# AdaLN and FFN adapters: a fixed first adapter, its first pieces and A's rows loaded in parts, ScalarE's small transfers later

## The chip, the cores and the metric

The kernel runs on one core of a Trainium2 chip. The metric is the device time of one execution in microseconds (us); lower is better. TensorE (PE in the profile) multiplies matrices, VectorE is DVE, ScalarE ACT, GpSimd POOL, and SyncE (SP) only issues transfers. A queue such as SPq or ACTq is the part of an engine that issues transfers and loads registers.

## The reference

For 64 samples of 64 tokens and 1024 features, two layers are applied, each added to its input:

```python
# layer 0
h = einsum('bct,bcd->bdt', x, L0_cond_weights[ids_0_15])       # mixes a sample's 64 tokens
y = h @ W_base.T + b_base + top-2-of-8 routed rank-16 adapters(h)
x = x + y
# layer 1
g = einsum('bsi,boi->bso', x, L1_cond_weight[ids_3_7])         # one of 8 matrices of 1024 x 1024 for each sample
z = 16 * sum over 8 heads of softmax(g @ Wr.T + br)[h] * (g @ A[h].T) @ B[h].T   # H = 8, scaling 2
x = x + z
```

Layer 1 never needs g itself: it needs g @ A.T and g @ Wr.T. So the kernel computes, once for each adapter in use, the product of [A; Wr] (136 rows of 1024) and the adapter's 1024 x 1024 matrix. This is the fold. The adapter numbers lie between 3 and 7, so five of eight are in use.

## The kernel before, in words

**The fold** (the first 82 us). The work on an adapter is cut in KC = 8 pieces. Piece c needs 512 KB of weights, `w1[KC*e + c]`, in the staging slot `stage[:, c, :]`, and all of [A; Wr]'s rows, `ag1_raw` (544 KB, eight blocks `oc` of 136 columns). TensorE makes 8 matmuls for it, one for each oc, with 128 columns of the piece and block oc of `ag1_raw` (`fold`, L391 to L403); in the trace each is two instructions. They sum in one of BANKS = 4 PSUM banks, and `unit_done` counts finished pieces (it starts at 8). ScalarE copies each result twice (`take_unit`, L629): rounded into `adapter` and unrounded into `hg`, then counts `unit_copied` (it starts at 4). TensorE waits at piece c for `unit_copied` >= 8n + c + 1, that is, for the copy of the piece four earlier. GpSimd subtracts one from the other to get the low part (L1065, `folded_lo`), and after four pieces ScalarE waits for that and stores the half adapter to device memory, `folded` (`take_adapter`, L638 to L645, signalled by `folded_stored`). The copies of the next adapter wait for these stores.

**Which adapters, in which order.** The first is the adapter of sample 0, read from `ids` by SP and ScalarE (`first_adapter`, L236). While it is folded, VectorE works out the list of the others in 14 short steps (L741 to L765, `plan_step`); every engine then reads how many there are and loops over them (`adapters_in_use`, L229, `adapter_at`, L233, each a register load).

**SP's order** (L342 to L372): the adapter ids, [A; Wr]'s rows whole, the register load of the first adapter, piece 0 in two halves (semaphores `first_landed` and `unit_landed[0]`), pieces 1 to 7, a wait for ScalarE's three small transfers (`small_landed`), then in the loop each piece once TensorE is done with its slot. After the fold's pieces come x of round 0, four of the eight mixing weights (`load_wc`), g0, the base weights in halves, and the turned x.

**ScalarE's order** (L620 to L698): three small transfers (condition ids, `br` and the bias, 0.2 to 4 KB), the load of its function table with one small exp, a wait for the three, four mixing weights `load_wc` (each a register load from `ids` and a transfer of 16 KB), then the first adapter's copies and stores, then the loop.

**TensorE** (L541 to L548) starts with WARM = 24 transposes of the identity matrix, waits for [A; Wr]'s rows, and folds. Behind the fold stand the mixing of round 0 (`mix`, L415), the gates, and eight rounds of the two layers.

Of the kernel before, what the change touches and what calls it, by code (L numbers as in the profile page):

```python
# [9 lines left out]
F32 = mybir.dt.float32  # L10
# [7 lines left out]
P = 128  # L18
SAMPLES = 64
CH = 64  # L20
D = 1024
KC = D // P
TOKENS = SAMPLES * CH
T = 512
# [4 lines left out]
EXPERTS = 8  # L29
RANK = 16  # L30
HR = EXPERTS * RANK
HG = HR + EXPERTS
# [3 lines left out]
BANKS = 4  # L36
SLOTS = 3
HALF = KC // 2
WARM = 24
REST = 4  # L40


# [5 lines left out]
def build(nc, x, x_turned, cond_ids, adapter_ids, w_cond, w0, g0, bias, b0, w1, ag1, b1, br, folded, out):  # L48
    with ExitStack() as ctx:
# [6 lines left out]
        def sem(name):  # L56
            return ctx.enter_context(nc.semaphore(name))
# [32 lines left out]
        adapter = sb("adapter", [P, SLOTS, KC, 2, HG], F32R)  # L90
# [12 lines left out]
        bias_cols = sb("bias_cols", [P, KC], F32)  # L103
        br_rows = sb("br_rows", [P, EXPERTS], F32)
        expert_no = sb("expert_no", [P, EXPERTS], F32)
        ids = sb("ids", [1, 2 * SAMPLES], I32)
# [48 lines left out]

        ids_landed = sem("ids_landed")
        small_landed = sem("small_landed")
        ag1_landed = sem("ag1_landed")
        first_landed = sem("first_landed")
        unit_landed = [sem(f"unit_landed{s}") for s in range(STAGE)]  # L160
        unit_done = sem("unit_done")
        unit_copied = sem("unit_copied")
# [69 lines left out]

        def adapter_at(eng, n):  # L233
            return eng.value_load(plan[0:1, bass.ds(n, 1)], min_val=0, max_val=EXPERTS - 1)

        def first_adapter(eng):  # L236
            eng.wait_ge(ids_landed, 16)
            return eng.value_load(ids[0:1, SAMPLES:SAMPLES + 1], min_val=0, max_val=EXPERTS - 1)

        def tail_out(n):  # L240

# [3 lines left out]
        def load_wc(eng, q, r, samples=range(PER)):  # L245

            for i in samples:
                no = eng.value_load(ids[0:1, bass.ds(at(q, r, PER, i), 1)], min_val=0, max_val=CONDS - 1)
                half = slice((i % 2) * CH, (i % 2 + 1) * CH)
                eng.dma_start(wc[half, i // 2, half], w_cond[bass.ds(no, 1), :, :].rearrange("a p n -> (a p) n")  # L250
                              ).then_inc(wc_landed, 16)
# [35 lines left out]
        def _(sp):  # L287
            def load_unit(e, c):
                sp.dma_start(stage[:, c, :], w1[bass.ds(KC * e + c, 1), :, :].rearrange("a p n -> (a p) n")
                             ).then_inc(unit_landed[c], 16)  # L290

            def load_x(q, r):
                for t in range(TILES):
                    sp.dma_start(x_rows[:, t, :], x[bass.ds(at(q, r, TILES, t), 1), :, :].rearrange("a p n -> (a p) n")
                                 ).then_inc(x_landed, 16)
# [43 lines left out]
                    load_xT(q, r + 1, 0)  # L339
                    load_xT(q, r + 1, 1)  # L340

            sp.dma_start(ids[:, SAMPLES:], adapter_ids).then_inc(ids_landed, 16)  # L342
            sp.dma_start(ag1_raw[:, :, :].rearrange("p k n -> p (k n)"), ag1).then_inc(ag1_landed, 16)
            e = first_adapter(sp)

            piece = w1[bass.ds(KC * e, 1), :, :].rearrange("a p n -> (a p) n")
            sp.dma_start(stage[:, 0, 0:T], piece[:, 0:T]).then_inc(first_landed, 16)
            sp.dma_start(stage[:, 0, T:D], piece[:, T:D]).then_inc(unit_landed[0], 16)
            for c in range(1, KC):
                load_unit(e, c)  # L350
            sp.wait_ge(small_landed, 48)
            total = adapters_in_use(sp)
            with sp.Fori(1, total) as n:
                e = adapter_at(sp, n)
                for c in range(KC):
                    sp.wait_ge(unit_done, KC * n + c + 1)
                    load_unit(e, c)
            load_x(0, 0)
            load_wc(sp, 0, 0, range(HALF, PER))
            sp.dma_start(g_raw[:, :, 1, :], g0).then_inc(g_landed, 16)  # L360
            for k in range(KC):
# [23 lines left out]
        def _(pe):  # L385
# [4 lines left out]

            def fold(n):  # L391
                for c in range(KC):
                    if c == 0 and isinstance(n, int):
                        pe.wait_ge(first_landed, 16)
                    else:
                        pe.wait_ge(unit_landed[c], 16 * n + 16)
                    pe.wait_ge(unit_copied, KC * n + c + 1)
                    for oc in range(KC):
                        if c == 0 and oc == HALF and isinstance(n, int):
                            pe.wait_ge(unit_landed[0], 16)  # L400
                        mm = pe.matmul(base_ps[c % BANKS][:, 0:HG], stage[:, c, oc * P:(oc + 1) * P],  # L401
                                       ag1_raw[:, oc, :], start=(oc == 0), stop=(oc == KC - 1))
                    mm.then_inc(unit_done, 1)  # L403
# [137 lines left out]
            pe.wait_ge(const_set, 5)  # L541
            for _ in range(WARM):
                pe.transpose(mix_ps[0][:, 0:P], identity[:, :], identity[:, :])
            pe.wait_ge(ag1_landed, 16)
            fold(0)
            total = adapters_in_use(pe)
            with pe.Fori(1, total) as n:
# [69 lines left out]

        @block.scalar
        def _(act):
            act.dma_start(ids[:, 0:SAMPLES], cond_ids).then_inc(small_landed, 16)  # L620
            act.dma_start(br_rows[:, :], br.partition_broadcast(P)).then_inc(small_landed, 16)
            act.dma_start(bias_cols[:, :], bias).then_inc(small_landed, 16)

            act.wait_ge(const_set, 5)
            act.activation(one_col[:, :], identity[:, 0:1], ACT.Exp)
            act.wait_ge(small_landed, 48)
            load_wc(act, 0, 0, range(HALF))

            def take_unit(n, c, again):  # L629
                act.wait_ge(unit_done, KC * n + c + 1 + STAGE)  # L630
                if again:
                    act.wait_ge(folded_stored[c // HALF], 16 * n)
                if again or c >= 4:
                    act.wait_ge(folded_lo, KC * n + c - 3)
                act.copy(adapter[:, 0, c, 0, :], base_ps[c % BANKS][:, 0:HG])
                act.copy(hg[:, c % 4, :], base_ps[c % BANKS][:, 0:HG]).then_inc(unit_copied, 1)

            def take_adapter(n, e, again):  # L638
                for p in range(2):
                    half = slice(p * HALF, (p + 1) * HALF)  # L640
                    for c in range(p * HALF, (p + 1) * HALF):
                        take_unit(n, c, again)
                    act.wait_ge(folded_lo, KC * n + (p + 1) * HALF)
                    act.dma_start(folded[bass.ds(e, 1), :, half, :, :].rearrange("a p k h n -> (a p) k h n").bitcast(F32),
                                  adapter[:, 0, half, :, :].bitcast(F32)).then_inc(folded_stored[p], 16)  # L645

            def yT_high(q, r, k):
                act.wait_ge(yT_done, at(q, r, KC, k + 1))
# [40 lines left out]
                if l1:  # L689
                    lwT_high(q, r - 1, on_pe=on_pe)  # L690

            e = first_adapter(act)
            take_adapter(0, e, False)
            total = adapters_in_use(act)
            with act.Fori(1, total) as n:
                e = adapter_at(act, n)
                take_adapter(n, e, True)
            iteration(0, 0, l1=False)  # L698
            with act.Fori(0, (ROUNDS - 2) // 2) as q:
                for r in (1, 2):  # L700
# [18 lines left out]
        def _(dve):  # L719
# [12 lines left out]
            def plan_after(instruction, step):  # L732
                instruction.then_inc(plan_step, 1)
                dve.wait_ge(plan_step, step)
# [10 lines left out]
            plan_after(dve.reduce_max(used[:, :], asks[:, :, :], AX.X), 3)  # L745


            plan_after(dve.tensor_scalar(not_first[:, :], expert_no[0:1, :], ids_f[:, 0:1], None,
                                         ALU.not_equal), 4)
            plan_after(dve.tensor_tensor(used[:, :], used[:, :], not_first[:, :], ALU.mult), 5)  # L750
            plan_after(dve.tensor_tensor(lower[:, :, :], e_cols, e_rows, ALU.is_le), 6)
# [419 lines left out]
```

## Time and profile before

| what | us |
|---|---|
| median of 3 runs (719.87 to 720.83) | 720.71 |
| the profiled execution, its own time | 720.81 |
| its span in the trace | 719.1 |
| TensorE busy | 711.3 |
| VectorE, ScalarE, GpSimd busy | 402.1, 115.7, 57.8 |

The trace's times count from the start of the span; the execution's own time is 1.7 us longer, for what lies around it. A line of the timeline has the start, the duration, engine, line of the source, operation, written and read tiles and the number of instructions; times of merged lines run from the first start to the last end. The chain of waits is followed back from the end of a stretch: at each step to what released it.

### The profile page before, as it was taken

What the parts mean: (1) busy time and instruction counts of PE and PEld (TensorE: products, weight loads), DVE (VectorE), ACT (ScalarE), POOL (GpSimd) and SP (SyncE); (2) the same over time, 40 slices, a digit from 0 to 9 for tenths busy, and PEclk for the clock granted to TensorE, in tenths of its full rate; (3) what the DMA queues carried; (4) which work ended last, traced back from release to release, by engine and by line L of the source; (5) the groups of instructions that cost most, each with busy time, mean ns of one, the idle gap of its engine ahead of it and who ended that gap; (6) DMA issues with size and microseconds to landing.
All of it is one profiled execution on the core that took longest, in us unless ns stands there. A gap on an engine that the chain in (4) does not pass through costs nothing.

```text
span 719.1 us, 12198 instructions
## 1 busy us (share of the span) xinstructions
PE 711.3 (99%) x4448; PEld 638.3 (89%) x4448; DVE 402.1 (56%) x1092; ACT 115.7 (16%) x312; POOL 57.8 (8%) x115
## 2 busy tenths in 40 slices
PE   8999999999999999999999999999999999999998
PEld 8999987898889988898889888998889888989997
DVE  2000298067846576466826784657646782685544
ACT  2222300031103110021003110311002100320111
POOL 1222310001100000001000110000000100010100
PEclk9999999999999999999999999999999999999999
DMA  8999993406755377428724674547742872386462
GB/s 301 413 369 345 390 412 105 170 5 207 250 197 198 124 230 268 172 80 302 278 113 151 210 255 190 196 129 230 263 175 76 303 273 118 147 304 222 180 249 88
DMA packets 38340, 156.26 MB, mean 217 GB/s; under 512 B 8852, under 2 KB 10900, under 8 KB 28052
## 3 DMA queue, kind: packets, MB, share of 16 engines
q1 hardware_dynamic: 27026, 78.66, 29.0%
q0 software_dynamic: 9216, 71.31, 28.8%
q10 hardware_dynamic: 2050, 5.65, 2.0%
q8 instruction: 32, 0.52, 0.3%
q14 instruction: 16, 0.13, 0.1%
HBM read 133.24 MB, written 22.35 MB: 216 GB/s over the span
## 4 chain that ended last, share of the span: by engine, by line
PE 92%; DVE 5%; DMA 2%; issue 1%; SPq 0%; ACT 0%; POOLq 0%; DVEq 0%
PE base_ps L387 17%; PE base_ps L388 17%; PE base_ps L389 17%; PE base_ps L401 10%; PE low_ps L461 4%; PE out_ps L461 4%; PE mix_both L415 4%; PE mix_both L426 3%; PE out_ps L415 2%; PE low_ps L415 2%; DVE w_lo L772 1%; PE low_ps L426 1%; PE out_ps L426 1%; DMA adapter<-folded 1%; PE mix_both L428 1%; PE low_ps L387 1%
## 5 line engine op out<-in xcount | busy, mean ns | idle before, releaser
L387 PE MATMUL base_ps<-yT,w_hi 128*128 128x512 f32 (+1 forms) x576 | 212.4, 369 | 0.7 <-DVE xT L916 0.5
L389 PE MATMUL base_ps<-yT,w_hi 128*128 128x512 f32 (+1 forms) x576 | 211.5, 367 | 0.0
L388 PE MATMUL base_ps<-yT,w_lo 128*128 128x512 f32 (+1 forms) x576 | 211.5, 367 | 0.0
L387 PEld LDWEIGHTS base_ps<-yT,w_hi 128*128 128x128 f32 x576 | 108.6, 188 | 20.7 <-DVE xT L916 2.7
L389 PEld LDWEIGHTS base_ps<-yT,w_hi 128*128 128x128 f32 x576 | 108.5, 188 | 17.8
L388 PEld LDWEIGHTS base_ps<-yT,w_lo 128*128 128x128 f32 x576 | 108.5, 188 | 16.0
L1079 POOL DMA_DIRECT2D adapter<-folded x60 | 31.9, 532 | 555.1 <-PE low_ps L461 482.8
L401 PE MATMUL base_ps<-ag_raw,stage 128*128 128x136 f32 x640 | 74.6, 280 | 0.6 <-DMA stage<-in_w 0.5
L401 PEld LDWEIGHTS base_ps<-ag_raw,stage 128*128 128x128 f32 x640 | 74.3, 190 | 1.0 <-DMA stage<-in_w 0.7
L776 DVE TENSOR_TENSOR yT<-mix_both,yT 128x512 fp32r<-128x512 f32 x32 | 22.0, 691 | 87.9 <-ACT yT L649 87.9
L955 DVE TENSOR_TENSOR xT<-xT,low_ps 128x512 f32<-128x512 f32 (+1 forms) x31 | 20.5, 662 | 87.9 <-PE low_ps L389 87.9
L788 DVE TENSOR_TENSOR x1T<-xT,x1T 128x256 fp32r<-128x256 f32 x120 | 45.4, 420 | 38.4 <-ACT x1T L656 38.4
L656 ACT CAST x1T<-xT 128x256 fp32r<-128x256 f32 x120 | 42.0, 405 | 135.1 <-PE out_ps L461 62.7
L916 DVE SCALAR_TENSOR_TENSOR xT<-base_ps,bias_cols,xT 128x512 f32<-128x512 f32 (+1 forms) x72 | 45.0, 685 | 29.2 <-PE base_ps L389 28.7
L649 ACT CAST yT<-mix_both 128x512 fp32r<-128x512 f32 x32 | 18.6, 585 | 176.5 <-PE mix_both L415 175.3
L461 PEld LDWEIGHTS out_ps<-adapter,x1T 128*128 128x128 f32 x240 | 33.3, 188 | 2.8 <-DMA adapter<-folded 0.9
L461 PEld LDWEIGHTS low_ps<-adapter,x1T 128*128 128x128 f32 x240 | 33.3, 188 | 2.8 <-DMA adapter<-folded 0.9
L461 PE MATMUL out_ps<-adapter,x1T 128*128 128x272 f32 x240 | 35.0, 288 | 0.7 <-DMA adapter<-folded 0.7
L461 PE MATMUL low_ps<-adapter,x1T 128*128 128x272 f32 x240 | 35.0, 288 | 0.5 <-DMA adapter<-folded 0.4
L881 DVE STREAM_TRANSPOSE hg<-rows 32x128 f32<-32x128 f32 x112 | 33.9, 303 | 1.8
L426 PE MATMUL mix_both<-g_hl,yT 128*128 128x272 f32 x128 | 31.5, 340 | 0.0
L415 PE MATMUL mix_both<-wc,x_rows 128*128 128x128 f32 x256 | 31.2, 275 | 0.0
(197 smaller groups left out, 904.8 us busy)
## 6 DMA issues: line engine op xcount, KB each, us to landing
adapter<-folded POOLq DMA_DIRECT2D x63, 1088.0 KB, 5.5
stage<-in_w SPq DMA_DIRECT2D x39, 512.0 KB, 6.3
x_rows<-in_x SPq DMA_DIRECT2D x32, 512.0 KB, 8.7
xT<-in_x_turned SPq DMA_DIRECT2D x16, 1024.0 KB, 6.0
out<-xT SPq DMA_DIRECT2D x28, 512.0 KB, 2.7
folded<-adapter ACTq DMA_DIRECT2D x10, 544.0 KB, 6.4
w_raw<-in_w SPq DMA_DIRECT2D x8, 256.0 KB, 6.8
w_raw<-in_w SPq DMA_DIRECT2D x4, 512.0 KB, 12.6
```

What stands on the lines that cost most here:

```text
L387: pe.matmul(dst, st_hi, mv_lo, start=start, stop=False, skip_group_check=True)
L388: pe.matmul(dst, st_lo, mv_hi, start=False, stop=False, skip_group_check=True)
L389: return pe.matmul(dst, st_hi, mv_hi, start=False, stop=stop, skip_group_check=True)
L401: mm = pe.matmul(base_ps[c % BANKS][:, 0:HG], stage[:, c, oc * P:(oc + 1) * P], ag1_raw[:, oc, :], start=(oc == 0), stop=(oc == KC - 1))
L415: mm = pe.matmul(hg_banks[k % 4][:, t * P:(t + 1) * P], x_rows[:, t, k * P:(k + 1) * P], wc[:, t, :], start=True, stop=True, skip_group_ch ...
L426: pe.matmul(hg_banks[t][:, 0:2 * HG], yT[:, 0, k, tile], g_hl[:, k, :, :].rearrange("p h n -> p (h n)"), start=(k == 0), stop=False, skip_ ...
L461: mm = pe.matmul(bank[:, 0:2 * HG], x1T[:, i % 2, k, :, :].rearrange("p h n -> p (h n)"), adapter[:, i % SLOTS, k, :, :].rearrange("p h n ...
L656: act.copy(x1T[:, i % 2, p * HALF:(p + 1) * HALF, 0, :], xT[:, half_of(r, p), :, i * CH:(i + 1) * CH]).then_inc(x1T_hi_done, 1)
L788: dve.tensor_tensor(x1T[:, i % 2, half, 1, :], xT[:, half_of(r, p), :, i * CH:(i + 1) * CH], x1T[:, i % 2, half, 0, :], ALU.subtract).then ...
L881: block_turned = dve.transpose(turned[rank:rank + BLOCK, :, tok:tok + BLOCK], rows[tok:tok + BLOCK, :, rank:rank + BLOCK])
L916: dve.scalar_tensor_tensor(row, base_ps[n % HALF][:, bank], bias_cols[:, n:n + 1], row, ALU.add, ALU.add).then_inc(x1_done, 1)
L1079: pool.dma_start(adapter[:, i % SLOTS, :, :, :], folded[bass.ds(e, 1), :, :, :, :].rearrange("a p k h n -> (a p) k h n")).then_inc(adapter ...
```

## The change

The first adapter is the constant `FIRST` = 4 in place of the adapter of sample 0, so nobody reads a register for it, and VectorE's plan leaves out that number. Piece 0 is loaded in four parts of 256 columns, piece 1 in two of 512 (`PARTS`), with a semaphore for each. [A; Wr]'s rows are loaded in four parts, by ScalarE in place of SP; TensorE waits part by part. The adapter ids are loaded by ScalarE behind them. ScalarE's three small transfers move from its start to between the two halves of the first adapter, and its wait for them and its four mixing weights to behind the second half, ahead of the loop. SP's wait for the small transfers moves behind the load of x. WARM falls from 24 to 7. The diff, cut to its core:

```diff
-WARM = 24
+WARM = 7
+FIRST = EXPERTS // 2
+PARTS = (4, 2)
...
-        def first_adapter(eng):
-            eng.wait_ge(ids_landed, 16)
-            return eng.value_load(ids[0:1, SAMPLES:SAMPLES + 1], min_val=0, max_val=EXPERTS - 1)
...
-            sp.dma_start(ids[:, SAMPLES:], adapter_ids).then_inc(ids_landed, 16)
-            sp.dma_start(ag1_raw[:, :, :].rearrange("p k n -> p (k n)"), ag1).then_inc(ag1_landed, 16)
-            e = first_adapter(sp)
-
-            piece = w1[bass.ds(KC * e, 1), :, :].rearrange("a p n -> (a p) n")
-            sp.dma_start(stage[:, 0, 0:T], piece[:, 0:T]).then_inc(first_landed, 16)
-            sp.dma_start(stage[:, 0, T:D], piece[:, T:D]).then_inc(unit_landed[0], 16)
-            for c in range(1, KC):
-                load_unit(e, c)
-            sp.wait_ge(small_landed, 48)
+            for c, many in enumerate(PARTS):
+                for p in range(many):
+                    cols = slice(p * D // many, (p + 1) * D // many)
+                    sp.dma_start(stage[:, c, cols], w1[KC * FIRST + c, :, cols]
+                                 ).then_inc(part_landed[c][p] if p < many - 1 else unit_landed[c], 16)
+            for c in range(len(PARTS), KC):
+                load_unit(FIRST, c)
...
             load_x(0, 0)
+            sp.wait_ge(small_landed, 48)
             load_wc(sp, 0, 0, range(HALF, PER))
...
                 for c in range(KC):
-                    if c == 0 and isinstance(n, int):
-                        pe.wait_ge(first_landed, 16)
-                    else:
-                        pe.wait_ge(unit_landed[c], 16 * n + 16)
+                    many = PARTS[c] if isinstance(n, int) and c < len(PARTS) else 1
                     pe.wait_ge(unit_copied, KC * n + c + 1)
                     for oc in range(KC):
-                        if c == 0 and oc == HALF and isinstance(n, int):
-                            pe.wait_ge(unit_landed[0], 16)
+                        if oc % (KC // many) == 0:
+                            p = oc // (KC // many)
+                            if p < many - 1:
+                                pe.wait_ge(part_landed[c][p], 16)
+                            else:
+                                pe.wait_ge(unit_landed[c], 16 * n + 16)
+                            if many == PARTS[0]:
+                                pe.wait_ge(ag1_landed[p], 16)
...
-            pe.wait_ge(ag1_landed, 16)
             fold(0)
...
-            act.dma_start(ids[:, 0:SAMPLES], cond_ids).then_inc(small_landed, 16)
-            act.dma_start(br_rows[:, :], br.partition_broadcast(P)).then_inc(small_landed, 16)
-            act.dma_start(bias_cols[:, :], bias).then_inc(small_landed, 16)
+            for p in range(PARTS[0]):
+                two = KC // PARTS[0]
+                act.dma_start(ag1_raw[:, p * two:(p + 1) * two, :].rearrange("p k n -> p (k n)"),
+                              ag1[:, p * two * HG:(p + 1) * two * HG]).then_inc(ag1_landed[p], 16)
+            act.dma_start(ids[:, SAMPLES:], adapter_ids).then_inc(ids_landed, 16)
...
-            act.wait_ge(small_landed, 48)
-            load_wc(act, 0, 0, range(HALF))
...
-            e = first_adapter(act)
-            take_adapter(0, e, False)
+            take_half(0, FIRST, 0, False)
+
+            act.dma_start(ids[:, 0:SAMPLES], cond_ids).then_inc(small_landed, 16)
+            act.dma_start(br_rows[:, :], br.partition_broadcast(P)).then_inc(small_landed, 16)
+            act.dma_start(bias_cols[:, :], bias).then_inc(small_landed, 16)
+            take_half(0, FIRST, 1, False)
+            act.wait_ge(small_landed, 48)
+            load_wc(act, 0, 0, range(HALF))
             total = adapters_in_use(act)
             with act.Fori(1, total) as n:
                 e = adapter_at(act, n)
-                take_adapter(n, e, True)
+                for p in range(2):
+                    take_half(n, e, p, True)
...
-            plan_after(dve.tensor_scalar(not_first[:, :], expert_no[0:1, :], ids_f[:, 0:1], None,
+            plan_after(dve.tensor_scalar(not_first[:, :], expert_no[0:1, :], float(FIRST), None,
                                          ALU.not_equal), 4)
```

`take_half(n, e, p, again)` is the body of the old `take_adapter` for one half p: four pieces, the wait for `folded_lo`, the store.

## Rows read from the trace of the kernel before

**Rows 1.** The page, its header and TensorE's busy time

```profile
span 719.1 us, 12198 instructions
...
PE 711.3 (99%) x4448; PEld 638.3 (89%) x4448; DVE 402.1 (56%) x1092; ACT 115.7 (16%) x312; POOL 57.8 (8%) x115
```

**Rows 2.** The chain of waits, first 130 us: start, duration, what it was

```profile
0.91 1.40 DMA ids<-in_adapter_ids
...
3.29 0.36 SPq L347
...
4.38 5.21 DMA stage<-in_w
9.63 72.55 PE base_ps L401 x624
...
89.98 0.69 DVE yT L776
```

**Rows 3.** The timeline of the first 30 us

```profile
1.32 0.39 SPq L343 DMA_DIRECT2D ag_raw<-in_ag  x1
...
1.88 0.45 ACTq L622 DMA_DIRECT2D bias_cols<-in_bias  x1
...
2.15 4.80 PE L543 MATMUL mix_both<-identity 128*128 128x128 f32 x24 [2.15 <-POOL identity L1059]
...
6.39 0.16 DVE L765 CAST plan<-x_rows 1x9 int32<-1x9 f32 x1
...
7.06 2.09 PE L401 MATMUL base_ps<-ag_raw,stage 128*128 128x136 f32 x16
```

**Rows 4.** TensorE's warming transposes (L543) by stretch

```profile
4.15:6.15 2.00, 2.00 (x11) 2.00 (x10) 1.00 0.77 215
6.15:6.95 0.80, 0.80 (x7) 0.56 (x5) 1.00 1.13 269
```

**Rows 5.** The transfer of A's rows (L343), time to landing

```profile
DMA to landing us min/median/max: 3.5/3.5/3.5
```

**Rows 6.** DMA by stretch (TensorE counts of L543); last number is GB/s

```profile
7.00:9.00 2.00, 0.00 (x0) 0.00 (x0) 1.00 0.87 298
9.00:11.00 2.00, 0.00 (x0) 0.00 (x0) 1.00 0.98 385
```

**Rows 7.** The transfer of piece 2 (L289), issued at 4.9

```profile
L289 SPq DMA_DIRECT2D stage<-in_w x1: 333/333/333, 4.9 to 4.9; - x1
...
DMA to landing us min/median/max: 6.3/6.3/6.3
```

**Rows 8.** The timeline from 70 to 82 us, SP's mixing weights

```profile
71.34 4.33 SPq L250 DMA_DIRECT2D wc<-in_w_cond  x4
```

**Rows 9.** Who SP's queue waited for: total us, times, longest

```profile
SPq L289 <- PE base_ps L401: 35.6, 29, 1.5
```

**Rows 10.** ScalarE on the timeline of the first 32 us

```profile
6.20 4.18 ACTq L250 DMA_DIRECT2D wc<-in_w_cond  x4
...
15.50 0.27 ACT L635 CAST adapter<-base_ps 128x136 fp32r<-128x136 f32 x1 [1.41 <-PE base_ps L401]
...
16.66 0.38 ACTq L644 DMA_DIRECT2D folded<-adapter  x1
...
24.42 0.36 ACTq L644 DMA_DIRECT2D folded<-adapter  x1
26.76 0.27 ACT L635 CAST adapter<-base_ps 128x136 fp32r<-128x136 f32 x1 [3.40 <-PE base_ps L401]
...
27.09 0.29 ACT L635 CAST adapter<-base_ps 128x136 fp32r<-128x136 f32 x1
```

**Rows 11.** The register loads of the mixing weights (L248)

```profile
L248 ACTq TENSOR_LOAD <-ids x4: 278/288/482, 5.3 to 9.2; - x4
```

**Rows 12.** ScalarE's mixing weights (L250), time to landing

```profile
DMA to landing us min/median/max: 6.0/6.2/6.5
```

**Rows 13.** ScalarE's stores (L644), time to landing

```profile
DMA to landing us min/median/max: 5.8/6.4/8.1
```

More of the change, by code:

```diff
@@ L157, in build @@
         small_landed = sem("small_landed")
-        ag1_landed = sem("ag1_landed")
-        first_landed = sem("first_landed")
+        ag1_landed = [sem(f"ag1_landed{p}") for p in range(PARTS[0])]
+        part_landed = [[sem(f"part_landed{c}_{p}") for p in range(many - 1)] for c, many in enumerate(PARTS)]
         unit_landed = [sem(f"unit_landed{s}") for s in range(STAGE)]
@@ L636, in take_unit, with take_half @@
                 act.copy(hg[:, c % 4, :], base_ps[c % BANKS][:, 0:HG]).then_inc(unit_copied, 1)
[L638 to L645, printed above, removed]
+            def take_half(n, e, p, again):
+                half = slice(p * HALF, (p + 1) * HALF)
+                for c in range(p * HALF, (p + 1) * HALF):
+                    take_unit(n, c, again)
+                act.wait_ge(folded_lo, KC * n + (p + 1) * HALF)
+                act.dma_start(folded[bass.ds(e, 1), :, half, :, :].rearrange("a p k h n -> (a p) k h n").bitcast(F32),
+                              adapter[:, 0, half, :, :].bitcast(F32)).then_inc(folded_stored[p], 16)
             def yT_high(q, r, k):
```

## The prediction

> **What bounds the kernel now.** I read the page first: TensorE is busy for 99% of the span, so only work in front of it or a hole in it can move the time [rows 1]. Then the chain of waits for the first 130 us, because the edit touches the fold at the head alone [rows 2]. It runs: the adapter ids' transfer, SP's register load, the two halves of piece 0, the transfer of piece 1 (issued 4.38, landed 9.59), then 624 fold matmuls without a pause for 72.55 us, from 9.63 to about 82.2, then the mixing matmuls and, from 89.98, VectorE. Each fold matmul takes 72.55 / 624 = 0.1163 us, a piece (8 matmuls, each two instructions) 1.86 us. So piece k starts at 9.63 + 1.86 (k - 1): piece 2 at 11.49, piece 8 at 22.65, which I call T7, the moment at which piece 7 is done. What counts is when this unbroken run starts, and whether something breaks it.
>
> The timeline shows the head [rows 3]: 24 transposes from 2.15 to 6.95, piece 0 from 7.06 to 9.15, then a wait for piece 1. The clock column says full speed (1.00), but the instructions don't: in the two windows [rows 4], 11 start in 2.00 us (with the ten before them 0.213 us apart, the 1.2 GHz level) and then 7 in 0.80 us (0.11 us apart, the 2.4 GHz level). The engine had been busy for some 4 us, from 2.15 to about 6.1, when it rose.
>
> **Start: what comes earlier.** Today SP issues the first weights at 3.29, behind the ids (0.91), A's rows (1.32) and the register load [rows 2, 3]. With a fixed adapter SP issues weights from 0.91, and ScalarE A's rows from 0.9; an issue costs 0.39 to 0.45 us on either engine [rows 3], so the eight parts are out by about 2.4 and the two halves of piece 1 by 3.3.
>
> When they land is a question of rate. A's rows, 557 KB, landed 3.5 us after issue [rows 5]; in the window from 7 to 9 us the core received 298 GB/s, from 9 to 11 us 385 [rows 6]. At 300 GB/s the 557 KB take 1.9 us, which leaves 1.6 us that don't depend on size. So N bytes land at 0.91 + 1.6 + N / 300 GB/s: the first parts (270 KB) at 3.4, piece 0 with all of A's rows (1.08 MB) at 6.1, piece 1 (1.61 MB) at 7.9, piece 2 (2.13 MB) at 9.6; from there pieces come every 1.4 us, faster than 1.86. I take piece 2 starting at 9.65 in place of 11.49: **1.8 us gained**.
>
> The bounds. Below: piece 2 is issued at 4.90 and lands 6.3 us later, at 11.2, that is 7.9 us after the first weights' issue, with 1.57 MB between. A's rows now share this stream; with another 1.4 us for their bytes piece 2 would land at 0.91 + 9.3 = 10.2 and the gain is 1.2 us [rows 2, 7]. Above: TensorE itself. Seven transposes end at 2.15 + 7 x 0.213 = 3.64; from 3.7 until 6.05 some 10 instructions run at the slow level (0.227 us each, 0.213 scaled by 136 / 128 columns), the other 22 of pieces 0 and 1 at 0.116: piece 2 could start at 8.6, a gain of 2.9 us.
>
> The Trainium skill (DMA: Bandwidth & Descriptors, Issuing engines are not separate DMA queues) says that transfers started by ScalarE and SyncE run on the same 16 DMA engines, and that using both saves issue time only. By that rule A's rows don't come for free beside the weights, which is how the sum is made; with both streams free of each other it would take the upper bound, 2.9.
>
> **The 17 transposes** removed cost nothing: parts of piece 0 run at the slow level in their place.
>
> **The ids and the plan.** Adapter ids are issued fifth on ScalarE, about 2.8, behind 1.6 MB, and land near 8; the 14 steps of the plan (4.2 us, from the ids' landing at 2.3 to 6.39 + 0.16 today) then end near 12.2 [rows 2, 3], SP's register loads near 13.5. Piece 8's load, which waits for the plan and for piece 0, goes out at about 13.5. TensorE needs it at T7, now 20.8, and pieces 4 to 7 still keep the DMA busy until about 15.5, so this costs 0. Cover gone, it would cost 1 us per us once the plan is later than about 15. SP's own wait for the small transfers, moved behind the load of x, ends long before. Its mixing weights go out from 71.34 to 75.67 [rows 8], behind the pieces, whose loads wait for TensorE 29 times [rows 9]: they move with TensorE, and with a landing time near 6.2 us they keep their 0.8 us ahead of the mixing. The rest of the span follows TensorE's end of the fold, and moves with it.
>
> **ScalarE: what is put in the way.** Today its four mixing-weight transfers stand ahead of the first piece (6.20 to 10.38) [rows 10], and TensorE waits for none of it. After the change they stand between its store of pieces 4 to 7 and its copy of piece 8. From T7:
> - copies of piece 7 and GpSimd's subtraction, as after piece 3 (copy 15.50, store issued 16.66), then the issue: 0.26 + 1.16 + 0.36 = 1.8 us [rows 10]
> - four samples, each a register load and an issue: first load 0.48, from 5.3 to 10.38 [rows 10, 11]: 5.0 us
> - two register loads for the count and the adapter and the loop's entry: 24.78 to 26.76 [rows 10], 2.0 us
> - the two copies of piece 8: 0.45 us
> Together 9.2 us. TensorE has four banks: piece 12 needs the bank of piece 8, and it is due at T7 + 4 x 1.86 = 7.4 us. **A hole of 1.8 us** opens in front of piece 12. Behind it ScalarE needs 0.33 us a piece (26.76 to the next at 27.09) and catches up, so it opens once.
>
> To this comes the wait for the small transfers themselves. Piece 3 is done 7.4 us before T7; the store goes out 1.45 us after it, the last of the three small ones 2.9 us after it. ScalarE asks for them at T7 + 1.8, 6.3 us after the last issue. ScalarE's transfers of today land in 6.0 to 6.5 us [rows 12], its stores in 5.8 to 8.1 [rows 13], and the three lie behind one such store. I add 0.3 us, with 0 and 1.8 as ends. A hole of 2.1 us; between 1.3 (the two register loads at 0.28 us each like a sample's [rows 11], with the loop's entry 1.5 in place of 2.0) and 3.6. The three issues themselves (1.3 us) lie in front of piece 4's copy, which TensorE needs only 7.4 us later: 0.
>
> **The sum:** -1.8 + 2.1 = +0.3 us on the profiled execution, whose span is 719.1 and whose time is 720.81, 0.1 above the median of 720.71. I predict **720.9 us**. What a measurement can tell apart here is 0.2%, 1.4 us, so this is no change.
>
> **The rivals.**
> - *No hole* (0.22). ScalarE's series is shorter than it looks or TensorE isn't held by the bank; then the start's gain stands: 720.8 - 1.8 = 719.0, and at the start's bound 717.9. For it: the chain never shows ScalarE in the fold. Against: 9.2 us against 7.4, nearly all from durations of the same instructions.
> - *The small transfers are late* (0.14), slower. Place: ScalarE's wait behind its second store. It decides from 6.3 us of landing time on, and every us beyond it lengthens the hole by one. At 8.1 us, the slowest store, the hole is 3.6 and the time 720.8 - 1.8 + 3.6 = 722.6; the top of the range, 723.0, is reached at 8.5 us.
> - *TensorE's clock stays low* (0.10), slower. The pauses between parts could keep the 1.2 GHz level. From 3.7 us on, piece 2 is reached by 9.65 if the clock rises by 8.1; later than that each us costs half. Never rising before piece 2, 32 instructions x 0.227 end at 11.0, the start gains 0.5, and the time is 722.4. Against: four us of work were enough before, and the parts come about as fast as they are used.
> The Trainium skill (TensorE: Matmul & The Clock Gate, Part 1: The HAM clock gate) says that the slow clock is the default and that activity releases it; the trace agrees with its rise at 6.1 us, and by this rule an engine that pauses more at the start could keep the slow level, as in this rival.
> - *The start at its upper bound, with the hole*: 720.8 - 2.9 + 2.1 = 720.0, inside the forecast.
>
> **How the numbers follow.** Forecast 0.54, rivals 0.22, 0.14, 0.10. The forecast's own range is 719.4 (2.9 against 1.5) to 722.4 (1.2 against 2.8). Reaching into the others until 2 in 10 are outside gives 718.9 to 723.0. Faster by over 1.4 us: the first rival and 0.03 of the forecast, 0.25. Slower: the second and most of the third, 0.22. The rest 0.53.
>
> **What would show it.** First fold matmul at 3.7 to 4; piece 2 near 9.65; SP's issue of piece 8 near 13.5; ScalarE's four wc issues between the second store and piece 8's copy; one gap of about 2 us in the fold, released by ScalarE, near T7 + 7.4 (28 us); end of the fold within 1.4 us of 82.2. I am wrong if the fold has no such gap, or if it starts later than 10.2 or earlier than 8.6 with piece 2.

## The result, and the profile after

The changed kernel is **slower**: 725.68 us (median of 6 runs, 724.99 to 727.91) against 720.34 us (6 runs), a measured ratio of 1.0081 with a 95% interval of 1.0069 to 1.0092 (the quotient of the two medians is 1.0074). That is 5.3 us more; the forecast was 720.9 and its range ended at 723.0. The profiled execution took 725.72 us, its span is 724.1 us. Three executions of the kernel before, taken beside the experiments, lasted 2225 to 2534 us and are left out of all medians.

The chain of waits of the changed kernel's first 40 us, with start, duration and what it was; the last two lines are from the same view of the first 130 us:

```profile
6.92 0.73 PE base_ps L402 x4
7.65 6.54 PE base_ps L402 x52
...
14.73 0.48 POOL adapter L1070
15.24 0.38 ACTq L642
...
15.65 0.30 ACTq L692
15.98 0.34 ACTq L693
16.35 9.14 DMA bias_cols<-in_bias
25.52 0.78 ACTq L248
...
30.36 0.48 ACTq L250
```

```profile
33.20 53.78 PE base_ps L402 x448
86.98 1.78 PE mix_both L416 x16
```

Before, this chain was one run of matmuls from 9.63 on [rows 2]. Now it leaves TensorE after piece 3, goes through ScalarE's first store and its three small transfers (L692 to L694), waits 9.1 us for the last of them, the bias, then through four register loads and issues (L248, L250), the two register loads of the loop and piece 8's copies, and only then back to TensorE at 33.20. The mixing begins at 86.98, against 82.18 before (9.63 + 72.55): 4.8 of the 5 us of span are lost in the fold.

TensorE's timeline on both sides of the hole, with the idle time and what ended it in brackets:

```profile
24.78 4.22 PE L402 MATMUL base_ps<-ag_raw,stage 128*128 128x136 f32 x35
33.20 3.97 PE L402 MATMUL base_ps<-ag_raw,stage 128*128 128x136 f32 x18 [4.21 <-ACT hg L635]
```

The pause is 4.2 us, in front of piece 12. ScalarE's side of it, to be read against [rows 10]:

```profile
22.65 0.35 ACTq L642 DMA_DIRECT2D folded<-adapter  x1
26.71 4.13 ACTq L250 DMA_DIRECT2D wc<-in_w_cond  x4
32.70 0.27 ACT L634 CAST adapter<-base_ps 128x136 fp32r<-128x136 f32 x1 [10.63 <-issue]
```

The 18 matmuls after the pause took 3.97 us, twice what they should. The windows before, in and behind it (columns: stretch, its length, TensorE's busy time and number of matmuls, then weight loads, VectorE, ScalarE, GpSimd, the granted clock, DMA share, GB/s):

```profile
28.90:33.10 4.20, 0.10 (x1) 0.00 (x0) 0.00 (x0) 0.40 (x3) 0.00 (x0) 1.00 1.03 405
33.20:36.50 3.30, 3.30 (x14) 3.30 (x15) 0.00 (x0) 1.01 (x6) 1.76 (x4) 0.50 0.40 145
36.60:39.90 3.30, 3.30 (x30) 3.30 (x30) 0.00 (x0) 0.89 (x4) 0.94 (x2) 1.00 0.68 254
```

Behind the pause the granted clock is 0.50, the 1.2 GHz level: 14 matmuls in 3.30 us, and 30 in the next 3.30. The 16 missing would have taken 1.9 us at the full level; over the whole run behind the pause, 448 x 0.1163 = 52.1 us would have been enough where 53.78 were taken, so the stretch costs about 1.7.

The sum of the fold: piece 12 was due at 9.63 + 11 x 1.86 = 30.1 before. Here the matmuls in front of the pause end at 29.00; by the engine's pace (24.78 + 35 x 0.1163) piece 12 was due at 28.85: **1.2 us gained** at the start. It came at 33.20: **4.35 us lost** to the hole, and 1.7 to the clock. -1.2 + 4.35 + 1.7 = 4.85, against 4.8 seen.

### The profile page after: what moved, and what is told of

It reads as the page before. It is cut to its first block, busy times and chain, and to the rows that moved or that the text cites. A ratio compares the mean times of both kernels' runs of the same rounds, so it can differ in the third digit from the quotient of the medians.

```text
span 724.1 us, 12172 instructions
## 1 busy us (share of the span) xinstructions
PE 711.7 (98%) x4431; PEld 637.7 (88%) x4431; DVE 402.1 (56%) x1092; ACT 115.7 (16%) x312; POOL 57.7 (8%) x115
## 4 chain that ended last, share of the span: by engine, by line
PE 90%; DVE 4%; DMA 3%; ACTq 1%; issue 1%; ACT 0%; SPq 0%; POOL 0%; POOLq 0%; DVEq 0%
PE base_ps L385 17%; PE base_ps L386 17%; PE base_ps L387 17%; PE base_ps L402 8%; PE low_ps L462 4%; PE out_ps L462 4%; PE mix_both L416 4%; PE mix_both L427 3%; PE out_ps L416 2%; PE low_ps L416 2%; DVE w_lo L777 1%; PE out_ps L427 1%; PE low_ps L427 1%; DMA bias_cols<-in_bias 1%; DMA adapter<-folded 1%; PE mix_both L429 1%
## 5 line engine op out<-in xcount | busy, mean ns | idle before, releaser
L402 PE MATMUL base_ps<-ag_raw,stage 128*128 128x136 f32 x640 | 78.0, 285 | 5.0 <-ACT hg L635 4.2
L402 PEld LDWEIGHTS base_ps<-ag_raw,stage 128*128 128x128 f32 x640 | 77.0, 195 | 6.3 <-ACT hg L635 4.4
```

## The experiments

Each is a change to the changed kernel, or to the experiment named. Each was compared with the kernel before on the same chip: e1 to e4 on one, e5 to e8 on a second, e9 to e12 on a third, where the kernel before had medians of 719.88, 719.65 and 719.78 us (720.34 beside the changed kernel). Medians of different groups can differ by some tenths for that alone.

| run | median us | ratio to before, 95% interval |
|---|---|---|
| changed kernel | 725.68 | 1.0081 (1.0069 to 1.0092) |
| e1, mixing weights on SP | 720.48 | 1.0007 (0.9992 to 1.0023) |
| e2, small transfers at the head | 721.54 | 1.0024 (1.0008 to 1.0041) |
| e3, head as before | 721.41 | 1.0017 (1.0004 to 1.0030) |
| e4, 20 transposes | 724.75 | 1.0067 (1.0046 to 1.0088) |
| e5, e1 with 24 warming | 720.07 | 1.0002 (0.9992 to 1.0011) |
| e6, e1 filled | 719.85 | 0.9997 (0.9987 to 1.0006) |
| e7, mixing weights among pieces | 719.23 | 0.9998 (0.9985 to 1.0012) |
| e8, small ones ahead of the store | 721.13 | 1.0023 (1.0013 to 1.0033) |
| e9, 38 transposes | 724.65 | 1.0060 (1.0041 to 1.0078) |
| e10, e7 with coarse parts | 719.60 | 0.9997 (0.9988 to 1.0006) |
| e11, e7 filled | 718.81 | 0.9985 (0.9976 to 0.9994) |
| e12, e8 with two samples | 719.91 | 0.9998 (0.9989 to 1.0007) |

### Is the hole ScalarE's series? (e1, e3, e7)

e1:

```diff
             take_half(0, FIRST, 1, False)
-            act.wait_ge(small_landed, 48)
-            load_wc(act, 0, 0, range(HALF))
...
-            load_wc(sp, 0, 0, range(HALF, PER))
+            load_wc(sp, 0, 0)
```

> The changed kernel, but ScalarE's four mixing-weight transfers and its wait for the small transfers are taken out of its order; SP issues all eight behind x. Theory 1 (the hole of 4.5 us in the fold is ScalarE's series between piece 7 and piece 8's copy): no hole, no time at 1.2 GHz behind it, the fold ends about 80.9 instead of 87.0, and with nothing late behind it 725.7 - 4.4 - 1.7 = 719.6. SP's queue is 5 us later for the base weights, which had 7.8 us to spare before the change. Rival (the later stages want the mixing weights early, or the start of the fold itself lost the time): 722 or more, with a wait for mixing weights in front of the mixing.

Measured: 720.48 us. The hole is gone. Two lines of e1's chain of waits of the first 100 us, and one of its waits:

```profile
6.30 59.38 PE base_ps L402 x504
...
81.24 2.02 PE mix_both L416 x16
```

```profile
PE mix_both L416 <- DMA wc<-in_w_cond: 0.7, 1, 0.7
```

TensorE waits for no copy of ScalarE in the fold, and the mixing begins at 81.24, 0.9 us earlier than before, after a wait of 0.7 us for the mixing weights that SP now sends late. The profiled execution took 719.75 us, as expected (719.6), but the median is 0.9 above that: the 12 runs lie between 719.4 and 722.7, four of them above 721.9. Theory 1 holds for the hole; the spread was new and led to e5 and e6.

e3 puts the three small transfers behind the adapter ids, and the wait and four mixing weights ahead of the first copy:

```diff
             act.dma_start(ids[:, SAMPLES:], adapter_ids).then_inc(ids_landed, 16)
+            act.dma_start(ids[:, 0:SAMPLES], cond_ids).then_inc(small_landed, 16)
+            act.dma_start(br_rows[:, :], br.partition_broadcast(P)).then_inc(small_landed, 16)
+            act.dma_start(bias_cols[:, :], bias).then_inc(small_landed, 16)
...
+            act.wait_ge(small_landed, 48)
+            load_wc(act, 0, 0, range(HALF))
             take_half(0, FIRST, 0, False)
```

> The changed kernel, with the small transfers at the head behind the adapter ids and the wait and the four mixing weights ahead of the first copy, as in the kernel before. Theory 1: no hole; the first copy near 12.7, before TensorE needs the bank of piece 0 at about 14; what is left is the gain of the start, 1.2 us: 719.1. Rival (the early start is worth nothing behind the fold, since transfers or VectorE bound there): 720.3.

Measured: 721.41 us, a miss of 2.3 us. Lines of its chain of waits, first 100 us, and of its waits:

```profile
4.01 7.21 DMA bias_cols<-in_bias
...
16.83 66.99 PE base_ps L402 x576
```

```profile
PE base_ps L402 <- ACT hg L638: 2.2, 1, 2.2
```

The place that cost nothing before costs a hole of 2.2 us here. The bias is issued at 4.01 behind A's rows and the ids, and lands 7.2 us later, at 11.2; the mixing weights follow until 16.3, and piece 4 waits for piece 0's copy until 16.83. Before, the small transfers were issued from 0.9 on, ahead of everything. The hole moved to another place: the same series, behind a transfer that was late again, met another bank.

e7 spreads the four over the second adapter's pieces; the second adapter's pass is written out ahead of the loop, which then begins at 2:

```diff
+            for p in range(2):
+                for c in range(p * HALF, (p + 1) * HALF):
+                    take_unit(1, c, True)
+                    if 2 <= c < 2 + HALF:
+                        if c == 2:
+                            act.wait_ge(small_landed, 48)
+                        load_wc(act, 0, 0, [c - 2])
...
+            with act.Fori(2, total) as n:
```

> The changed kernel, with ScalarE's wait for the small transfers and its four mixing weights taken out of the place ahead of the loop and put one by one behind the copies of pieces 2 to 5 of the second adapter. A register load and an issue are 1.2 us and the copies 0.45, together less than the 1.86 us of a piece. Theory 1 (the hole comes from four in a row and from the wait, not from the work as such): no hole in the fold, no late mixing either, so the fold ends at 80.3 and the median is that of e1 or up to 1 us better, 719.5 to 720.5, with e1's spread at the start. Rival (the work is a loss wherever it stands): a series of small holes and 722 or more.

Measured: 719.23 us. Its chain has the fold as one run:

```profile
7.08 74.32 PE base_ps L402 x632
81.40 1.78 PE mix_both L416 x16
```

No hole at all with the same register loads, issues and wait in the same queue. The work isn't the loss; four in a row are, with the wait ahead of them. (e7 spreads the four and also puts them later, when the small transfers have long landed; which of the two matters how much, e7 alone doesn't show.)

### How much is the wait for the small transfers? (e2, e8, e12)

e2 has e3's three lines at the head, but keeps the mixing weights ahead of the loop.

> The changed kernel, with the three small transfers issued at the head behind the adapter ids, the four mixing weights left in front of the loop. Theory 1 (2.5 us of the hole are the wait for the late small transfers, the rest the register loads and issues): the hole shrinks from 4.4 to about 1.9 us. If TensorE's clock falls only after a long pause, it stays up: 725.7 - 2.5 - 1.7 = 721.5; if it falls after 1.9 us too: 723.2. Rival (the wait is hidden anyway, the series itself is what is long): hole 4 us, 725.5.

Measured: 721.54 us, against 721.5. One line of its waits:

```profile
PE base_ps L402 <- ACT hg L638: 1.7, 1, 1.7
```

The pause is 1.7 us in place of 4.2, and the clock stays at 1.00 behind it. So the wait for the small transfers is 2.5 us of the hole, and the series that I had worked out (a hole of 1.8 us without the wait) is the rest. The agreement of the median is partly luck: the twelve runs fall in two groups, eight from 720.1 to 722.0 us and four from 723.5 to 724.2. The profiled execution (720.11 us) is the fastest of all, and the mean clocks of the upper four (0.999 and 1.0) show no stretch like the changed kernel's, so what those four lost isn't shown.

e8 moves the three only by one step, from behind the first store to in front of it:

```diff
+                if p == 0 and not again:
+                    act.dma_start(ids[:, 0:SAMPLES], cond_ids).then_inc(small_landed, 16)
+                    act.dma_start(br_rows[:, :], br.partition_broadcast(P)).then_inc(small_landed, 16)
+                    act.dma_start(bias_cols[:, :], bias).then_inc(small_landed, 16)
                 act.wait_ge(folded_lo, KC * n + (p + 1) * HALF)
                 act.dma_start(folded[bass.ds(e, 1), :, half, :, :]...
```

> The changed kernel, with the three small transfers issued ahead of the first store instead of behind it. In the changed kernel the last was issued at 16.35 and landed at 25.41, 9.1 us later. Theory 3 (they land late because they stand behind the 544 KB store on ScalarE's queue): they land about 2 us earlier after issue, 7 us, and the hole shrinks from 4.4 to about 2 us; with the clock up this gives 722. Rival (they wait for the transfers of all queues issued before, and the store is a small part of these): 8.5 us or more after issue, hole 3.5 to 4 us, 725.

Measured: 721.13 us, 4.5 us better than the changed kernel (about 4 when each is set against the kernel before beside it: 1.5 us slower here, 5.3 there). ScalarE's timeline at the same places, and the timeline of TensorE behind the hole:

```profile
14.68 0.45 ACTq L644 DMA_DIRECT2D bias_cols<-in_bias  x1
...
22.45 0.35 ACTq L646 DMA_DIRECT2D folded<-adapter  x1
23.75 4.50 ACTq L250 DMA_DIRECT2D wc<-in_w_cond  x4
30.12 0.27 ACT L634 CAST adapter<-base_ps 128x136 fp32r<-128x136 f32 x1 [8.26 <-issue]
```

```profile
30.62 6.64 PE L402 MATMUL base_ps<-ag_raw,stage 128*128 128x136 f32 x55 [1.83 <-ACT hg L635]
```

Between the end of the second store's issue (22.80) and the first mixing weight (23.75) there is 0.95 us, what one register load and its instructions take when there is no wait (5.3 to 6.20 before, 0.9; 0.95 in e2, where the small transfers were issued by 4.01). So the bias, issued at 14.68, was there by 22.8, at most 8.1 us later, against 9.1 behind the store. It is issued 1.7 us earlier and needs at least 1 us less: together the 2.5 us of wait are gone, and with the shorter pause (1.8 us) the clock stays up in this execution.

Theory 3 holds in its effect, but that the store makes the bias late isn't shown. The store itself, issued at 15.24 in the changed kernel, took 7.6 us, less than the bias behind it; the piece that SP issued at 16.2, beside the bias, took 8.9:

```profile
L289 SPq DMA_DIRECT2D stage<-in_w x1: 333/333/333, 16.2 to 16.2; - x1
...
DMA to landing us min/median/max: 8.9/8.9/8.9
```

In e8 the pieces issued at 14.3 and 14.9, on both sides of the bias, took 7.5 and 9.0 us; in e3 those issued at 3.8 and 4.3 took 6.8 and 7.6 us, and the bias between them 7.2. So each time the 4 KB transfer was about as late as a 512 KB piece issued at the same moment, with the store ahead of it or without, as the rival of e8's expectation has it (though its number, 8.5 us or more, was missed). Against this stand ScalarE's mixing weights of 16 KB, with no store just ahead: before they took 6.0 to 6.5 us [rows 12] while the pieces issued beside them took 8.0 to 10.2. e8 moves the bias both away from the store and 1.7 us earlier, so the runs don't decide; the cause of the 9.1 us stays open.

e12 gives two of e8's four samples to SP:

```diff
-            load_wc(act, 0, 0, range(HALF))
+            load_wc(act, 0, 0, range(2))
...
-            load_wc(sp, 0, 0, range(HALF, PER))
+            load_wc(sp, 0, 0, range(2, PER))
```

> The kernel with the small transfers ahead of the first store (e8), with two of ScalarE's four mixing weights given to SP. Theory (the remaining hole of 2.1 us is four register loads and issues of 1.2 us too many in a row): two fewer shorten ScalarE's series by 2.4 us, the hole is gone, the fold ends at 80.5 instead of 82.5 and the median is 721.1 - 2.1 = 719.0. SP's two more put its last mixing weight 2.4 us later, about 0.5 us late for the mixing at most. Rival (the hole follows from something else than the number of samples): 721.

Measured: 719.91 us, 1.2 us better than e8 where 2.1 were expected. The hole is gone (TensorE waits for no ScalarE copy in the fold). Yet the fold of the profiled execution ended at 82.43 and not at 80.5, for a reason that the last group of experiments shows (the slow level at its start):

```profile
6.87 75.56 PE base_ps L402 x632
```

### What does the clock cost? (e4, e9)

Both add transposes of the identity on TensorE ahead of the loop, 20 in e4 and 38 in e9, so that TensorE is busy while ScalarE is behind:

```diff
             fold(0)
+            for _ in range(20):
+                pe.transpose(mix_ps[0][:, 0:P], identity[:, :], identity[:, :])
```

> The changed kernel with 20 more transposes of the identity on TensorE between piece 7 and piece 8, 2.2 us of work that computes nothing. ScalarE's series doesn't depend on them, so piece 12 still starts near 33.2 and the pause is 2.2 instead of 4.4 us. If the long pause makes the clock fall: it stays at 2.4 GHz and the time falls by 1.7 us to 724.0 in spite of the added work. Rival (the pause alone is the loss, the clock costs nothing): 725.7; and if 2.2 us of pause are enough for a fall: 725.7 too, with the same half-speed stretch of 3.4 us in the records.

> The changed kernel with 38 more transposes between piece 7 and piece 8, 4.1 us of work that computes nothing. They nearly fill the pause of 4.5 us in front of piece 12, which is set by ScalarE and stays where it is. Theory (a pause of 4.5 us makes the clock fall to 1.2 GHz for 3.4 us or twice that, which costs 1.7 or 3.4 us): no low stretch in the records, every run's mean clock at 0.999 or above, median 723.5 to 724, 2 us below the changed kernel's, and no run above 725. Rival (the clock's fall doesn't cost time, since ScalarE is behind anyway): 725.7 as the changed kernel.

Measured: 724.75 and 724.65 us. The pause, the run behind it and the mixing's start, from the waits and the chains of e4 and then of e9:

```profile
PE base_ps L402 <- ACT hg L637: 2.3, 1, 2.3
```

```profile
33.58 52.16 PE base_ps L402 x448
85.74 1.78 PE mix_both L416 x16
```

```profile
PE base_ps L402 <- ACT hg L637: 0.5, 1, 0.5
```

```profile
33.49 52.16 PE base_ps L402 x448
85.65 1.78 PE mix_both L416 x16
```

With 2.2 or 4.1 us of useless work more, the mixing begins 1.2 and 1.3 us *earlier* than the changed kernel's 86.98, and in both profiles the clock is 1.00 behind the pause. The run of 448 instructions takes 52.16 us in both (and in e2 and e8), and 53.78 in the changed kernel: 1.6 us for the clock. So the rival, that the clock costs nothing, is out for the profiled executions.

The other executions show less. Each run has its mean granted clock: the changed kernel's six runs have 0.995 to 0.998 (3.4 us at half of 724 us make 0.998, two such stretches 0.995), e4 has 0.998 in two of ten, 726.9 and 728.6 us, the slowest, and e9 has 1.0 in all five. A mean doesn't say where the clock fell: of the 31 runs of the kernel before beside e1 to e4 one has 0.998 as well (724.44 us). Nor do the times follow the means closely: the changed kernel's three runs at 0.995 took 725.19, 726.52 and 727.91 us, the other three 724.99 to 725.72. Against the kernel before beside it, the changed kernel is 5.3 us slower, e4 and e9 4.9 each, where 2 us between them were expected for e9; two of e9's five runs are above 725, where none was expected, and the intervals overlap. So what the clock costs in the median isn't settled.

### Where does the spread come from? (e5, e6, e10, e11)

e5 is e1 with `WARM = 24`. e6 is e1 with `WARM = 9` and transposes in TensorE's pauses at piece 0:

```diff
-WARM = 7
+WARM = 9
...
+                        if isinstance(n, int) and c == 0:
+                            for _ in range({1: 1, 3: 4, 5: 1}.get(oc, 0)):
+                                pe.transpose(mix_ps[0][:, 0:P], identity[:, :], identity[:, :])
```

> The kernel with all mixing weights on SP (e1), with 24 warming transposes again in place of 7. TensorE is then busy without a pause from 2.15 until the fold. Theory 2 (in some executions the pauses between the first parts keep the clock at 1.2 GHz for longer, which is what spreads e1 from 719.4 to 722.7): the fold starts at 7.1, pieces 0 and 1 run at full speed behind each other, piece 2 starts at 10.8 in every execution, the times lie within 1 us like those of the kernel before, and the median is 720.5 or less. Rival (the spread comes from elsewhere): it stays at 3 us, and the median goes up by the 0.9 us that the start loses.

> The kernel with all mixing weights on SP (e1), with 9 warming transposes and 1, 4 and 1 more behind the first three parts of piece 0, where TensorE waited, so that it has hardly a pause before piece 1. Theory 2 (pauses keep the clock low in some executions): the clock rises by 9 us in all of them, the upper third of the times of e1 (722.0 to 722.7) is gone, and the median is 719.8. Rival (the pauses don't matter): the same spread of 3 us and 720.5.

Measured: e5 720.07 us, 9 of 11 runs between 719.15 and 720.23, two at 721.4 and 721.8; e6 719.85 us, 718.4 to 720.9, none above 721. e1's upper third is gone in both, but with some ten runs each, on another chip than e1's, that is a hint and no proof, and e5 kept a spread of 2.7 us where 1 was expected. No slow execution of e1 was profiled. What the traces show is that such a loss occurs. TensorE in four windows of e8's profiled execution, then of e12's (columns as above, TensorE alone):

```profile
2.15:4.00 1.85, 1.75 (x7) 1.00 0.88 282
4.00:8.00 4.00, 3.25 (x15) 1.00 1.00 312
8.00:11.00 3.00, 3.00 (x27) 1.00 1.02 415
```

```profile
4.00:8.00 4.00, 3.25 (x13) 1.00 0.93 297
8.00:11.00 3.00, 3.00 (x15) 1.00 1.02 416
11.00:14.00 3.00, 3.00 (x27) 1.00 1.03 422
```

The two kernels are the same up to here. In e8 TensorE makes 27 instructions between 8 and 11 us, the full level; in e12 15, and 27 only from 11 on. The clock column says 1.00 throughout: it doesn't show the level at the start. Twelve instructions fewer are 1.4 us, and e12's profiled execution (721.0 us) is 1.1 above its median. In this execution the rise came some 3 to 4 us later than in e8's. This is the third rival of the prediction, real but in some executions only: the changed kernel's profile has 10 or 11 instructions in each us from 8 on, e7's has 7 from 8 to 9, e10's 6 from 8 to 9 and 6 from 9 to 10. That the pauses between the parts are what delays the rise isn't shown: e10 works without a pause from 5.12 on, and rises late too.

e11 is e7 with e6's warming. e10 is e7 with fewer parts:

```diff
-PARTS = (4, 2)
+PARTS = (2, 1)
```

> e7 with e6's warming: 9 transposes and 1, 4 and 1 behind the first parts. Theory: both losses are gone, the hole and the late rise of the clock; piece 2 starts at 10.1 in every execution, against 11.5 before; the median is 718.9 and no run is above 721. Rival (the gain of the start is lost elsewhere): 719.7, as the kernel before.

> The kernel with the mixing weights behind the pieces of the second adapter (e7), with the parts of piece 0 and of A's rows two instead of four and piece 1 whole. Theory (the start is bound by the bytes of A's rows and pieces 0 and 1, so finer parts only fill TensorE's slow time): the first fold matmul starts near 5 instead of 4.4, piece 2 still at 10.2 to 10.8, median within 0.5 us of e7's 719.2. Rival (the parts are what makes the start early): piece 2 at 11.5, the median 1 us above e7's.

Measured: e11 718.81 us, no run above 719.8, the only kernel here that is faster than the one before beyond its interval: 0.9985, between 0.9976 and 0.9994. It is one of twelve comparisons, and e7, the same kernel without the filling, has 0.9998 on another chip, with an interval that overlaps; what the filling alone is worth isn't settled. Its windows:

```profile
4.00:8.00 4.00, 4.00 (x19) 1.00 1.00 344
8.00:11.00 3.00, 3.00 (x26) 1.00 1.03 419
```

TensorE never waits at the start, and the fold's last run (8.43 us, 72.74 us long) ends at 81.17, 1.0 us earlier than before; piece 2 starts near 10.8 (8.43 + 20 x 0.1163), where 10.1 was expected. e10: 719.60 us, within 0.4 of e7 as the first theory said, though its profiled execution took 723.81 us. In it piece 2 starts only near 11.5 (36 instructions stand between 5.12 and 12.0), where 10.2 to 10.8 was expected, because TensorE is at the slow level until after 10; the weights weren't late, piece 2 was issued at 2.8 and landed at 10.0. From 4 to 6 us this core received 417 GB/s, against 281 with the finer parts of the changed kernel, whose piece 2 landed no earlier (10.1). In these two profiles the finer parts came with a slower stream, which the theory didn't have.

The same execution shows a fall of the clock in another place, behind a pause of 1.8 us and 1.3 us of work:

```profile
650.88 1.27 PE L462 MATMUL out_ps<-adapter,x1T 128*128 128x272 f32 x8 [1.79 <-DMA adapter<-folded]
```

```profile
651.00:652.20 1.20, 1.20 (x10) 1.00 1.07 435
652.30:655.60 3.30, 3.30 (x17) 0.50 0.62 192
655.70:659.00 3.30, 3.30 (x30) 1.00 1.03 382
```

## Why the prediction was wrong

- **The start.** Right within its bounds: 1.2 us were gained, my lower bound, not 1.8. The step that failed is the rate: TensorE waited for the third and fourth part until 6.92 and 7.65, where I had piece 0 complete at 6.1, and piece 2, which I had at 9.6, was issued at 3.77 and landed at 10.1:

```profile
L289 SPq DMA_DIRECT2D stage<-in_w x1: 432/432/432, 3.8 to 3.8; - x1
...
DMA to landing us min/median/max: 6.3/6.3/6.3
```

It started near 10.25 (28.85 - 10 x 1.86). The formula with 300 GB/s and one fixed cost was too fast (the core received 278 to 281 GB/s until 6 us); the bound from piece 2's landing [rows 7] was the better estimate. The Trainium skill (DMA: Bandwidth & Descriptors, Issuing engines are not separate DMA queues) says that what the two queues start runs on the same 16 DMA engines. The trace agrees, with the gain at 1.2 us and not at the 2.9 of streams free of each other.

- **The 17 transposes.** Costed at nothing. In the profiled execution they were; in e12's the slow level lasted until 11 us, 1.4 us more than in e8's. I had this as a rival with 0.10.
- **The ids and the plan.** Right, and a us early: the plan ended at 10.70 (12.2 forecast), SP issued piece 8 at 12.5 (13.5). SP's queue waited 3.6 us for the plan, and nobody for SP.
- **ScalarE's series.** Right: 9.2 us without the wait in the changed kernel as well, so 1.8 us of hole; e2 and e8 have pauses of 1.7 and 1.8 us.
- **The wait for the small transfers.** The term that failed first. I took 0.3 us, with 1.8 as its end, from the 6.0 to 6.5 us of today's small transfers and the 5.8 to 8.1 us of stores [rows 12, 13]. It measured 2.5: the transfer took 9.1 us. The step that failed is the choice of rows: none of them is a small transfer issued close behind a store, and the range ended at the slowest store, 8.1. What makes it 9.1 stays open (e8). But the trace before had a slower transfer at the same moment; the pieces that SP issued at 13.8, 15.6 and 17.5 took 9.2, 9.0 and 8.4 us, and 9 us was the end to take. The middle one:

```profile
L289 SPq DMA_DIRECT2D stage<-in_w x1: 333/333/333, 15.6 to 15.6; - x1
...
DMA to landing us min/median/max: 9.0/9.0/9.0
```

The second rival had the place, the decision point of 6.3 us and the price of 1 us for each us; with 9.1 it gives a hole of 1.8 + 2.8 = 4.6, and 4.35 was seen (ScalarE asked 6.65 us after the last issue, not 6.3). I gave it 0.14.

- **The clock behind the hole.** Missing from the sum. I asked whether the clock would be low at the start and not what a pause of four us in the middle does. It costs 1.7 us in the profiled execution; the mean clocks of three of the six runs say that the slow time was up to twice as long there, but not where it stood. The Trainium skill (TensorE: Matmul & The Clock Gate, Part 1: The HAM clock gate) says that the slow clock is the default and comes back when the engine is idle. The trace agrees, with 0.50 for 3.4 us behind a pause of 4.2 us.
- **The rest of the span** followed the fold's end, as said: 636.9 us from the mixing's start to the end before, 637.1 after.

In all: -1.2 for -1.8, +4.35 for +2.1, +1.7 for 0: 4.85 in place of 0.3, and the profiled execution was 4.9 us longer (725.72 against 720.81). The recorded 720.9 is also 0.1 below its own sum (720.71 + 0.3), which changes nothing.

## What to carry to other kernels

Before moving work on an engine that only serves TensorE, lay its whole series from one release to the next against the number of free banks times the pace; single steps between the copies cost nothing here, four in a row cost 1.8 us, and with a late small transfer ahead of them 4.35. Let the range for a small transfer's landing end no earlier than that of the large ones issued at the same moment, and issue it long before its wait: one step here was worth about 4 us, the clock included. When a pause of TensorE is put into the sum, ask what the clock does behind it.

## What the runs showed of the hardware that was not expected

- A 4 KB transfer took 9.1 us from issue to landing at 16 us, and 7.2 us at 4 us (e3). Pieces of 512 KB issued beside it took 8.9 us, and 6.8 and 7.6 us; transfers of 16 KB took 6.0 to 6.5 us beside pieces of 8.0 to 10.2 (the kernel before). What decides isn't shown.
- Behind a pause of 4.2 us the granted clock was 0.50 for 3.4 us in the changed kernel's profile, and the mean clock says as much or up to twice that for all six runs. It stayed at 1.00 behind pauses of 2.3 us (e4's profile) and 1.8 us (e8's), but two of e4's ten runs have a mean of 0.998. In e10 it fell in the rounds, 1.3 us of work behind a pause of only 1.8 us, so the length of the last pause alone doesn't tell.
- The clock column can say 1.00 at the start while the instructions run at the 1.2 GHz level (15 instructions in 3 us in e12); there the spacing has to be read.
- The first weights came more slowly in fine parts: 281 GB/s from 4 to 6 us with parts of 256 columns, 417 with 512 (e10), one profile each.
